# A token-mixer norm moved from VectorE to ScalarE, and the addition of a leaving batch moved up in VectorE's order

## The reference

```python
    x = x + _L1_ffn_ref(_layernorm(x, axis=-1), ...)
    x = x + _L1_attn_b_ref(_layernorm(x, axis=-1), ...)
    x = x + _L1_ffn_ref(_layernorm(x, axis=-1), ...)
```

```python
        xn = _simple_rmsnorm(x)
        u = jax.nn.silu(jnp.einsum('nbe,de->nbd', xn, Wu) + bu)
        v = jax.nn.silu(jnp.einsum('nbe,de->nbd', xn, Wv) + bv)
        vh = v.transpose(1, 0, 2).reshape(b, n, H, HD).transpose(0, 2, 1, 3)
        oh = _toeplitz_causal_fft(vh, zero, pos)
        o = oh.transpose(0, 2, 1, 3).reshape(b, n, D1).transpose(1, 0, 2)
        o = u * o
        out = jnp.einsum('nbd,ed->nbe', o, Wo) + bo + shortcut
```

## Time and profile before

| | |
|---|---|
| median of 3 runs | 1547.79 us (1545.13 to 1552.1) |
| profiled execution, its own time | 1546.34 us |
| its span in the profile | 1544.6 us |
| busy over the span: PE, DVE, ACT, POOL | 84%, 67%, 53%, 55% |
| mean granted TensorE clock | 0.929 of full speed |
| last stage | about 1265 us to the end |

### The profile page before, as it was taken

The page is one execution under the profiler, slowest core; times in us unless marked ns, Lnnn a source line. Parts: engine busy times, 40 slices in busy tenths (PEclk is TensorE's granted clock), DMA queues, the critical chain, the costliest instruction groups (busy, mean ns, idle before and its releaser), DMA issues. The chain is left out here.

```text
span 1544.6 us, 33697 instructions
## 1 busy us (share of the span) xinstructions
PE 1290.3 (84%) x11257; PEld 837.3 (54%) x11257; DVE 1037.5 (67%) x3084; ACT 816.6 (53%) x1382; POOL 852.5 (55%) x1270
## 2 busy tenths in 40 slices
PE   5875899887999999878996588999999978875778
PEld 4665899732344444358995233344555546543456
DVE  5764555477888888735554788977666425766976
ACT  3642223213677777832331267877455547674675
POOL 4376655344346655655555678877433215655553
PEclk9986999998999999979997599999999988997899
DMA  8012222374333333322224000000000000000001
GB/s 245 13 40 69 81 69 70 84 150 110 76 76 90 88 86 87 99 80 77 79 73 137 1 2 1 2 1 2 1 2 2 2 1 1 2 0 1 1 1 56
DMA packets 86437, 79.41 MB, mean 51 GB/s; under 512 B 11791, under 2 KB 76175, under 8 KB 85968
## 3 DMA queue, kind: packets, MB, share of 16 engines
q1 hardware_dynamic: 72434, 55.07, 14.4%
q0 software_dynamic: 8640, 17.84, 3.5%
q10 hardware_dynamic: 5196, 4.35, 1.2%
HBM read 45.94 MB, written 31.28 MB: 50 GB/s over the span
## 5 line engine op out<-in xcount | busy, mean ns | idle before, releaser
L1459 ACT ACTIVATE grp_pt<-ps 128x1024 f32<-128x1024 f32 (+2 forms) x320 | 243.8, 800 | 171.3 <-PE ps L1538 89.7
L2487 DVE TENSOR_REDUCE soft_mx<-ps 128x2 f32<-128x1024 f32 (+3 forms) x256 | 199.4, 819 | 36.8 <-PE ps L2273 36.2
L2148 ACT ACTIVATE arena<-ps 128x768 f32<-128x768 f32 (+1 forms) x192 | 167.3, 881 | 81.6 <-PE ps L2306 68.9
L1039 POOL DMA_INDIRECT products<-moe_product,moe_rows_in x142 | 138.0, 972 | 123.6 <-DVE moe_product L1141 110.9
L1058 ACT ACTIVATE moe_hid<-ps 128x512 f32<-128x512 f32 x142 | 84.8, 597 | 203.2 <-PE ps L1089 201.6
L1089 PE MATMUL ps<-moe_rT,moe_W_now 128*128 128x128 f32 x1136 | 156.4, 282 | 11.3 <-issue 7.5
L2049 POOL TENSOR_SCALAR_AFFINE_SELECT arena<-arena 128x256 f32<-128x256 f32 (+1 forms) x192 | 92.3, 485 | 119.7 <-ACT arena L2148 118.0
L1089 PEld LDWEIGHTS ps<-moe_rT,moe_W_now 128*128 128x128 f32 x1136 | 143.3, 198 | 14.3 <-issue 10.4
L858 POOL DMA_INDIRECT sorted_rows<-route_row,route_target x128 | 129.0, 1008 | 34.2 <-issue 30.3
L1558 PE MATMUL ps<-grp_pt,grp_vpad 128*32 128x160 f32 (+4 forms) x2048 | 138.4, 378 | 2.9 <-POOL grp_pt L1400 2.9
L1400 POOL TENSOR_SCALAR_AFFINE_SELECT grp_pt<-grp_pt 128x256 f32<-128x256 f32 (+1 forms) x192 | 111.7, 594 | 34.7 <-ACT grp_pt L1459 33.3
(11 more groups left out here) (370 smaller groups left out, 2850.9 us busy)
## 6 DMA issues: line engine op xcount, KB each, us to landing
moe_rows_in<-sorted_rows SPq DMA_DIRECT2D x142, 65.0 KB, 1.9
route_stacks<-soft_scratch_k SPq DMA_DIRECT2D x32, 192.0 KB
arena<-products SPq DMA_DIRECT2D x8, 512.0 KB, 7.3
soft_scratch_q<-soft_parts SPq DMA_DIRECT2D x16, 192.0 KB, 2.8
route_stacks<-soft_scratch_q SPq DMA_DIRECT2D x32, 96.0 KB
arena<-products SPq DMA_DIRECT2D x4, 768.0 KB, 12.7
soft_scratch_k<-soft_parts SPq DMA_DIRECT2D x15, 192.0 KB, 2.8
products<-moe_product,moe_rows_in POOLq DMA_INDIRECT x142, 2.2
```

Source lines behind the costliest of these rows:

```text
L1039: pool.indirect_dma_start(k.products, bass.IndirectOffsetOnAxis(rows_in[:, s % RING, DEST_COL:DEST_COL + 1].bitcast(U32), 0), product[:, s ...
L1459: act.activation(at.pair(pt[:, s % 2, :], pair, seg)[:, :, 0:w], ring[(chunks_before(m) + c) % 2][:, :, 0:w], ACT.Exp, scale=scale).then_i ...
L2148: act.activation(LATENT.pair(pt[:, s % 2, :], pair, seg)[:, :, 0:w], ring[second_turn(n, c) % RING3][:, :, 0:w], ACT.Exp, scale=scale).the ...
L2487: ins = dve.tensor_reduce(mx[:, tile, half, :, r], ring[first_turn(n, d) % RING3][:, :, at:at + keys], AX.X, ALU.max)
```

## The change

It does three things, all in `tail`. First, VectorE adds a batch that leaves feed-forward 0 in the step in which TensorE turns it (t - 4), as the last thing ahead of the gate and the lag terms, and no longer at the start of the step after (t - 5), behind them. Batches that leave feed-forward 1 stay where they were. Second, `norm_mix` moves from VectorE to ScalarE, where it is an activation with the reciprocal deviation as scale and a shift as bias, in the same step m + 1, between `apply_mix` and `silu`. Third, GpSimd makes that shift (minus the mean, times the reciprocal deviation) with two more instructions on 128x4 elements right behind each `mix_rstd`.

```diff
+                pool.tensor_scalar(mix_minus[:, :], mix_mv[:, n % 2, :, 0], -1.0, None, ALU.mult).then_inc(mix_power.sem, 1)
+                pool.wait_ge(mix_power.sem, mix_power.at(n, 3))
+                pool.tensor_tensor(mix_shift[:, n % 2, :], mix_minus[:, :], mix_rstd[:, n % 2, :], ALU.mult).then_inc(mix_power.sem, 1)
...
+            def norm_mix(n):
+                act.wait_ge(mix_power.sem, mix_power.at(n, 4))
+                need(act, mix_normed2, mix_normed2.at(n - 2))
+                need(act, shortcut, shortcut.at(n - 2))
+                for j in range(T):
+                    ins = act.activation(normed[:, n % 2, j, :], k.x[:, n * T + j, :], ACT.Identity, bias=mix_shift[:, n % 2, j:j + 1],
+                                         scale=mix_rstd[:, n % 2, j:j + 1])
+                ins.then_inc(mix_normed.sem, 1)
...
                 if t - 2 in mixes:
                     apply_mix(mixes[t - 2])
+                if t - 1 in mixes:
+                    norm_mix(mixes[t - 1])
                 if t - 5 in mixes:
                     silu(mixes[t - 5])
...
-            def norm_mix(n):
-                dve.wait_ge(mix_power.sem, mix_power.at(n, 2))
-                need(dve, mix_normed2, mix_normed2.at(n - 2))
-                need(dve, shortcut, shortcut.at(n - 2))
-                for j in range(T):
-                    ins = dve.tensor_scalar(normed[:, n % 2, j, :], k.x[:, n * T + j, :], mix_mv[:, n % 2, j, 0:1], mix_rstd[:, n % 2, j:j + 1],
-                                            ALU.subtract, ALU.mult)
-                ins.then_inc(mix_normed.sem, 1)
...
-                if t - 5 in leaves:
+                if t - 5 in leaves and leaves[t - 5][0] == 1:
                     add_x(*leaves[t - 5])
...
-                if t - 1 in mixes:
-                    norm_mix(mixes[t - 1])
+                if t - 4 in leaves and leaves[t - 4][0] == 0:
+                    add_x(*leaves[t - 4])
```

More of the change, by code:

```diff
@@ L2647, in tail @@
         mix_rstd = st.sb("mix_rstd", [P, 2, T], F32)
+        mix_minus = st.sb("mix_minus", [P, T], F32)
+        mix_shift = st.sb("mix_shift", [P, 2, T], F32)
         mix_ms = st.sb("mix_ms", [P, T], F32)
@@ L2672, in tail @@
         mix_stats_done = st.counter("mix_stats", 2)
-        mix_power = st.counter("mix_power", 7)
+        mix_power = st.counter("mix_power", 9)
         mix_normed = st.counter("mix_normed")
@@ L2728, in mix_rstd_power @@
                 pool.tensor_tensor(mix_rstd[:, n % 2, :], mix_pin[:, :], minus_half[:, :], ALU.pow).then_inc(mix_power.sem, 1)
+                pool.tensor_scalar(mix_minus[:, :], mix_mv[:, n % 2, :, 0], -1.0, None, ALU.mult).then_inc(mix_power.sem, 1)
+                pool.wait_ge(mix_power.sem, mix_power.at(n, 3))
+                pool.tensor_tensor(mix_shift[:, n % 2, :], mix_minus[:, :], mix_rstd[:, n % 2, :], ALU.mult).then_inc(mix_power.sem, 1)
             def mix_rms_power(n):
-                pool.wait_ge(mix_power.sem, mix_power.at(n, 2))
+                pool.wait_ge(mix_power.sem, mix_power.at(n, 4))
                 pool.tensor_tensor(mix_ms[:, :], mix_mv[:, n % 2, :, 1], mix_rstd[:, n % 2, :], ALU.mult).then_inc(mix_power.sem, 1)
-                pool.wait_ge(mix_power.sem, mix_power.at(n, 3))
+                pool.wait_ge(mix_power.sem, mix_power.at(n, 5))
                 pool.tensor_tensor(mix_ms[:, :], mix_ms[:, :], mix_rstd[:, n % 2, :], ALU.mult).then_inc(mix_power.sem, 1)
-                pool.wait_ge(mix_power.sem, mix_power.at(n, 4))
+                pool.wait_ge(mix_power.sem, mix_power.at(n, 6))
                 pool.tensor_tensor(mix_ms[:, :], mix_ms[:, :], half[:, :], ALU.pow).then_inc(mix_power.sem, 1)
-                pool.wait_ge(mix_power.sem, mix_power.at(n, 5))
+                pool.wait_ge(mix_power.sem, mix_power.at(n, 7))
                 pool.tensor_scalar(mix_ms[:, :], mix_ms[:, :], 1e-8, None, ALU.add).then_inc(mix_power.sem, 1)
-                pool.wait_ge(mix_power.sem, mix_power.at(n, 6))
+                pool.wait_ge(mix_power.sem, mix_power.at(n, 8))
                 need(pool, mix_normed2, mix_normed2.at(n - 2))
```

## The result

| | before | after |
|---|---|---|
| median of 5 runs each | 1547.79 us (1545.13 to 1552.1) | 1539.12 us (1534.85 to 1541.15) |
| ratio, 95% interval | | 0.9937 [0.9914, 0.9960] |
| profiled execution, its span | 1546.34, 1544.6 us | 1534.85, 1533.1 us |
| mean granted clock | 0.929 | 0.929 |

The change makes the kernel faster by 0.6%: 8.7 us by the medians, 9.8 us by the ratio with an interval from 6.2 to 13.3. My forecast was 1541.4 us, 6.4 us less than before. The time lies in the range, and just beyond the line of 0.5% that I had put at 1540.05 us; the interval reaches to both sides of that line. The 1547.79 us of before, given ahead as the median of three runs, is that of five.

What follows compares the result with a forecast made beforehand. No one engine was taken to bound the last stage: waits fill its middle, VectorE bounds its end. Terms 0.4 - 1.1 - 4.6 - 1.1 = -6.4 us from the 1547.79 us median gave 1541.4 us, range 1535.5 to 1548.

Steps and rivals of the forecast that it cites:

- the line of 0.5%: Whole kernel: a change under 0.5% (7.7 us) can't be told from none; the line for faster is 1540.05 us.
- Term A: Steps 14 to 22: +0.4 us; batch 0's turn comes 2.5 us earlier, lost to GpSimd, ScalarE's norm and low clock.
- Term B: Steps 23 to 28: -1.1 us; batch 4's turn starts earlier, but batch 5's norm stands ahead of batch 3's SiLU.
- my 0.7: Last stage: 0.7 us gained by 1409 us; a gain not within 2 us of that would be wrong.
- Term C: Steps 29 and 30: -4.6 us; batch 7's `add_x` goes ahead of lag instructions, so TensorE turns batch 5 earlier.
- that sign of being wrong: Steps 29 and 30: ScalarE's SiLU ending last by more than a microsecond would show the prediction wrong.
- Term D: Steps 31 and 32: -1.1 us; batch 7's norm, 2.05 us, leaves VectorE, but TensorE's second product caps the gain.
- Behind step 32 no edit is left, and the rest follows unchanged: Last stage, after step 32: nothing more is gained or lost, 0 us.
- The first (larger gain, clock up): Last stage: clock stays up and norms lie in waits; -11.2 us, 1536.6 us, chance 0.2.
- The second (VectorE waits in its place): Last stage: VectorE waits for the turn-out in place of TensorE; -3.0 us, 1544.8 us, chance 0.2.
- The third (ScalarE the bound): Last stage: ScalarE becomes the bound and all eight norms cost 1.65 us; +6.7 us, 1554.5 us, chance 0.1.

Runs made afterwards that it cites:

- the first profile: No edit between the two: the changed kernel profiled first, 210.6 us from batch 0's turn-out to the end, and again on another chip, 211.2 us.
- batch 7 alone: Changed kernel with only batch 7 added early, the other seven where they were before: 213.2 us from batch 0's turn-out to the end, ratio 0.9964.
- the split: Changed kernel with norms of batches 0 to 4 on VectorE behind the addition, 5 to 7 on ScalarE behind the SiLU: ratio 0.9932.
- the split with the clock up: Changed kernel with norms divided between VectorE and ScalarE, plus zero-matrix products in TensorE's long waits: 1544.61 us, ratio 0.9850 to the kernel before.
- the zero products: Changed kernel with TensorE multiplying a zero matrix in five places where it waits long: ratio 0.9925; the same in the kernel before: 0.9964.
- the addition alone: Kernel before with the leaving batch added early, the norm staying on VectorE ahead of it: ratio 0.9938, 215.6 us from batch 0's turn-out to the end.

## Why the prediction was right

**Term A** came as forecast, by its own steps. The turn of batch 0 is at 1336.36, that is 1339.50 on the clock of before, where I had 1339.5. The projection ran at low clock, 3.78 us after 5.21 of waiting, for which I had 5.1. Two small errors in it cancel. GpSimd's price was too low, 0.7 us a batch and not 0.5, so its busy stretch up to the power that the scale needs grew by 1.4 us and not by about 1; and the way from ScalarE's scale to the SiLU was shorter than I had it, so that the SiLU came at 1351.9 instead of 1352.2.

**Term B** has the right mechanism and an uncertain size. The SiLU of batch 3 is at 1401.7 on the clock of before, where I had 1402.8; VectorE was idle 5.75 us ahead of the addition of batch 5 and not 7. In the first profile the term is -2.4 and in the second -0.7, around my -1.1; that the forecast lies between them is in part luck. By step 28, 1.9 and 0.2 us were gained, both within 2 us of my 0.7. The difference is the clock: TensorE's projections after the two waits took 3.35 and 3.38 us in the first, 3.78 and 3.78 in the second, and the products behind the last of them were slow in the second alone. I had given the low clock one price, 3.55 us, and no spread.

**Term C** was forecast as -4.6 and is -4.7 and -5.2, and with batch 7 alone -4.5. The wait of 8.90 us fell to 3.43, for which I had 4.4. These sizes are taken to the unit's addition in step 30. By the places that the prediction named, from the SiLU of batch 3 to `add_mixed` of batch 3, the term is -5.7 in the first profile and -4.2 in the second, and `add_mixed` comes at 1420.9 and 1422.9 on the clock of before, where I had 1423: the mechanism is sure, the size good to about 1 us. TensorE did not wait for ScalarE's SiLU of batch 4 here, so that sign of being wrong stayed away. This was the surest term because the profile showed both ends: an instruction that sat behind six others which nobody waited for, and what was late next.

**Term D** has the cap of the prediction, TensorE's second product, and not quite its size: -0.6 and -1.0 for -1.1. Before, that product ended 1.4 us ahead of the addition of step 32. I let 0.3 of that go to TensorE; measured from the addition of step 30, its end comes 0.8 us later in the first profile, where VectorE waited 0.43 us for it, and 0.4 in the second, where it ended as the addition began:

```profile
1462.87 1.02 PE L2879 MATMUL ps<-tail_yT,lin 128*128 128x512 f32 x2
...
1463.93 0.75 DVE L2965 SCALAR_TENSOR_TENSOR tail_h<-ps,pack,tail_h 128x512 f32<-128x512 f32 x1
```

VectorE's side of the term was wrong as well, without a price at this place. The 2.05 us of the norm did leave its row. But GpSimd's shortcut of batch 6, which had made the norm take 2.05, now meets the lag terms, which take 5.07 us where the same six took 4.06. The collision didn't go with the instruction that had suffered from it; it passed to the next. The Trainium skill ("SBUF — State Buffer", Who interferes with whom) says that VectorE and GpSimd share a port pair as an exclusive lock, held for a whole instruction, and that a VectorE instruction with two SBUF inputs contends for it with a GpSimd instruction that reads SBUF. The trace agrees: one of the six took 1.76 us beside the shortcut, and the others 0.74 or 0.75. By that rule I should have asked what would stand there next.

**What failed** is the sentence "Behind step 32 no edit is left, and the rest follows unchanged". 1.2 and 1.4 us were gained there, because ScalarE's wait for GpSimd, TensorE's idle time and then its clock in step 35 changed. With it the forecast would have been 1540.0 to 1540.2 us, at the line. It put at nothing a term that is a fifth of the forecast gain. All in all the stretch shrank by 8.3 and 7.7 us for a forecast of 6.4: the sum is short by a sixth to a quarter.

**The rivals.** The first (larger gain, clock up) did not come: the clock was low at all three projections. The second (VectorE waits in its place) holds in part: VectorE's wait for the turn-out is 9.0 us over five times, of which 5.75 is one, but the terms came out as forecast in spite of it. The third (ScalarE the bound) did not come: with the norms on VectorE the stretch is the same, though ScalarE has 13.2 us less to do. It isn't far, since one more set of norms costs 12.8 to 13.4 us. My reason against it, 19 of 60 us idle on ScalarE, was weak: idle time that lies in waits for others doesn't take up work that stands ahead of what others wait for.

The rule of the Trainium skill ("ScalarE: Activation LUTs", Rules for kernel authors) that I weighed, to leave adds and multiplies to VectorE, decides nothing here: VectorE and ScalarE give the same stretch (210.5 against 210.6 and 211.2), and the split with the clock up is better than either. On which engine the norm stands mattered less than what it stands ahead of.

**Still open.** Why the projection in step 35 keeps full clock after 2.35 us of idle time in one kernel and loses it after 1.94 in another; what differs ahead of it, no run isolates. Why the split and the zero products give 8 us together and at most 2 apart is only argued: a cause of low clock that is left in place gives back what the other edit won. Why the addition alone is 5 us behind in its stretch and level in its ratio is open as well; a second profile of it, and one of the kernel before on the same chip, would tell.

## What to carry to other kernels

Where several instructions of an in-order engine are ready, put first the one that another engine waits for: six lag terms ahead of one addition were worth 4.2 to 5.7 us, and the total of a wait (17.0 us) says little until one has read what is late next. To learn whether an engine has room at a place, double the operation there: with ScalarE busy for 76% of the time, 13.2 us of added norms cost 12.8 to 13.4. The reverse doesn't follow, since taking the norms off ScalarE gained nothing. Where waits are followed by a low clock, try an order once more with TensorE kept awake before it is judged, since the split was worth nothing without that and 6.7 us with it (209.2 to 202.5).

## What the runs showed of the hardware

- Four projections of 128x512 took 1.88 to 1.98 us at a granted clock of 1.00, which is 2.4 GHz, and 3.78 at 0.50, which is 1.2 GHz; times between the two come where the clock changed among them. A wait of 2.69 us was followed by 1.98 us in the kernel before and by 3.49 in the kernel with the addition alone, at the same place. The length of the last wait doesn't decide the level.
- Behind ten products with a zero matrix, 2.33 us, the granted clock was 1.00 across 2.34 us of idle time and in the projection after it.
- A collision of VectorE and GpSimd in SBUF cost VectorE about 1 us at both places that were read here: the norm 2.05 us for 1.1, six lag terms 5.07 for 4.06.
- Neighbouring activations of 128x128 with scale and bias overlap: each is 482 ns, four are 1.65 us.
